# A fused four-layer kernel: one decay matrix in the state-space stage, and another order of transposes in the last attention stage

## The reference, cut to what matters

```python
dt = jax.nn.softplus(dt + dt_bias)
xBC = jax.nn.silu(conv3(xBC))                       # x: 512 columns, B and C: 64 each
dA = jnp.exp(dt * -jnp.exp(A_log))                  # per token and head
h = h * dA_t[:, :, None, None] + dBx_t              # both directions
y = einsum('bhpn,bn->bhp', h, C_t)
y = shift(y_fw) + shift(y_bw) + x_og * (x_og @ fcD_w.T + Dp)
```

```python
q, k = q * cos + rotate_half(q) * sin, k * cos + rotate_half(k) * sin
att = softmax(causal(q @ k.T / sqrt(32)))
x = x + (att @ v) @ wo.T
probs = softmax(rmsnorm(x) @ router_w.T); tp, ti = top_k(probs, 2)
```

## Time and profile before

| | |
|---|---|
| median of 3 runs | 3548.52 us (3543.6 to 3556.27) |
| profiled execution | 3556.74 us, of which the span is 3555.0 us |
| mean granted TensorE clock | 0.89 |
| busy, share of the span | PE 77%, PEld 61%, DVE 65%, ACT 48%, POOL 27% |
| stage `ffn2` | from about 1429 us to 2225 us |
| stage `att3` | from about 2702 us to 3175 us |

### The profile page before, as it was taken

How to read it: one execution, slowest core, us unless ns; L and a number is a source line. 1 busy time by engine, 2 the same in 40 slices (tenths; PEclk the granted TensorE clock), 3 DMA queues, 4 the chain that set the end, 5 groups by cost and what they waited for, 6 DMA issues and landing times. The chain is left out here.

```text
span 3555.0 us, 69418 instructions
## 1 busy us (share of the span) xinstructions
PE 2741.3 (77%) x19770; PEld 2158.8 (61%) x19770; DVE 2322.4 (65%) x6747; ACT 1718.7 (48%) x4856; POOL 942.4 (27%) x908
## 2 busy tenths in 40 slices
PE   3999947973849608799999998688885777739993
PEld 2777737973749607566666666456552445429993
DVE  5777745647755575577777775688883767734555
ACT  1434415645636427444444442566662555516664
POOL 0232343650533414011111111000001233333442
PEclk9999978986869858899999998899996989859997
DMA  5121102324212232000000000100001000002225
GB/s 177 53 67 54 55 24 80 86 82 165 77 47 61 60 108 87 1 1 0 0 0 0 0 0 1 33 19 18 24 12 55 13 19 21 22 31 55 66 60 166
DMA packets 142549, 168.57 MB, mean 47 GB/s; under 512 B 19920, under 2 KB 118224, under 8 KB 141776
## 3 DMA queue, kind: packets, MB, share of 16 engines
q1 hardware_dynamic: 117744, 120.77, 11.3%
q0 software_dynamic: 21504, 44.74, 3.6%
q10 hardware_dynamic: 3168, 1.49, 0.2%
HBM read 115.87 MB, written 51.05 MB: 47 GB/s over the span
## 5 line engine op out<-in xcount | busy, mean ns | idle before, releaser
L1145 POOL DMA_INDIRECT y_rows<-ffn_e_rows_out,ffn_e_scatter_at x352 | 341.2, 969 | 435.5 <-DVE ffn_e_rows_out L1173 251.7
L1286 PE MATMUL bank<-ffn_e_xT,ffn_e_mine 128*128 128x128 f32 x3360 | 438.5, 278 | 2.2 <-ACT ffn_e_xT L1219 1.4
L1286 PEld LDWEIGHTS bank<-ffn_e_xT,ffn_e_mine 128*128 128x128 f32 x3360 | 409.2, 194 | 3.4 <-ACT ffn_e_xT L1219 2.2
L889 POOL DMA_INDIRECT sorted_rows<-ffn_r_h,ffn_r_slot x320 | 317.9, 994 | 320.3 <-issue 320.3
L1221 ACT ACTIVATE ffn_e_mine<-constants 128x512 f32 (+1 forms) x352 | 250.2, 712 | 126.2 <-issue 78.2
L1193 DVE TENSOR_TENSOR ffn_e_hid<-ffn_e_act,bank 128x256 f32<-128x256 f32 (+1 forms) x280 | 136.1, 486 | 224.0 <-ACT ffn_e_act L1246 185.5
L1296 PE MATMUL bank<-ffn_e_mine,ffn_e_hid 128*128 128x128 f32 x1968 | 278.1, 276 | 2.4 <-DVE ffn_e_hid L1197 2.1
L1296 PEld LDWEIGHTS bank<-ffn_e_mine,ffn_e_hid 128*128 128x128 f32 x1968 | 247.5, 192 | 5.4 <-DVE ffn_e_hid L1197 5.0
L2469 ACT ACTIVATE gnn_prob<-bank,gnn_low 128x256 f32<-128x256 f32 x512 | 193.9, 490 | 52.8 <-DVE gnn_low L2387 52.8
L2387 DVE TENSOR_REDUCE gnn_low<-bank 128x2 f32<-128x512 f32 x256 | 159.0, 683 | 63.6 <-PE bank L2563 63.5
L2575 PE MATMUL bank<-ident,gnn_prob 128*128 128x128 f32 x1024 | 146.2, 278 | 42.2 <-DVE gnn_probT L2398 31.7
(11 more groups left out here) (502 smaller groups left out, 6782.4 us busy)
## 6 DMA issues: line engine op xcount, KB each, us to landing
g_adj<-in_adjT SPq DMA_DIRECT2D x48, 512.0 KB, 3.9
ffn_e_rows_in<-sorted_rows SPq DMA_DIRECT2D x346, 66.0 KB
ffn_c_y<-y_rows SPq DMA_DIRECT2D x80, 256.0 KB, 3.3
g_adj_rows<-in_adj SPq DMA_DIRECT2D x16, 512.0 KB, 4.2
gnn_adj<-in_adjT SPq DMA_DIRECT2D x16, 512.0 KB, 3.8
constants<-in_ffn SPq DMA_DIRECT2D x1, 6281.0 KB, 17.8
y_rows<-ffn_e_rows_out,ffn_e_scatter_at POOLq DMA_INDIRECT x352, 2.2
constants<-in_ffn SPq DMA_DIRECT2D x1, 5206.0 KB, 15.9
```

Source lines behind the costliest of these rows:

```text
L889: g.indirect_dma_start(self.c.sorted_rows, bass.IndirectOffsetOnAxis(self.slot[par][:, k, j:j + 1], 0), self.h[par][:, j, :], None).then_i ...
L1145: g.indirect_dma_start(c.y_rows, bass.IndirectOffsetOnAxis(scatter_at[par][:, k:k + 1], 0), rows_out[par][:, k, :], None).then_inc(scatter ...
L1286: ins = pe.matmul(chunk(part, ch), chunk(weights[:, i * HALF:(i + 1) * HALF], ch), x, start=True, stop=True)
```

## The change

In `ffn2`: B and C are projected by one group of four products with 128 output rows, and their taps run on 128 partitions (`bc` is one tile, taps moved ahead of the softplus chain). The decay is multiplied in one matrix for both directions: `dt_run` (dt times the mask; the forward half by eight ScalarE copies, the backward half by one VectorE product of 1024 columns), `dt_both` (their sum), `g_both` (the two triangles of B.C added) and `factor` (their product). The exponential is taken head by head with minus A as its scale. The output takes 8 products with `xtok`. GpSimd no longer makes `a_run` and `xdt`, and its addition of the output bias waits for `norm_ps`. The logit pieces 2 and 3, the transposes, the four pieces of `tail_fin` (`fin_piece`) and the residual have other places.

In `att3`: the eight transposes are dealt out between other products on TensorE; the router's logits and ranks move to unused columns of bank 7, `PV[:, 320:384]` and `PV[:, 256:320]`; and the steps of all engines stand in another order. ScalarE's order now: the copy of hT, the exponentials of the first quad with its transpose 2 before the last of them, the copy of the outputs of quad 0, the router's rows, the rows of h, the router's exponential, the outputs of quad 1, v, and the exponentials of the second quad with transpose 2, the copy of onT and the router's hT between them.

```diff
+
+                    g.wait_ge(norm_ps, t * 2 + 1)
...
-                        g.wait_ge(dt_ready, t + 1)
...
-                        g.tensor_tensor(heads(xdt[d][:]), heads(xtok[:]), per_head(dt[:, d * HEADS2:(d + 1) * HEADS2], HD2),
...
+                    g.wait_ge(xtok_ready, t + 1)
...
+                    if more:
+                        soft_a(t + 1, 2)
                     tap_more(0, xpad, conv_x, xc, range(KC)).then_inc(xc_ready, 1)
+                    then(v, tap_last(bcpad, conv_bc, w["convb_bc"], bc, range(1)), conv, t * 4 + 3)
+                    then(v, tap_more(1, bcpad, conv_bc, bc, range(1)), conv, t * 4 + 4)
+                    tap_more(0, bcpad, conv_bc, bc, range(1)).then_inc(bc_ready, 1)
...
+                    v.tensor_tensor(dt_run[1][:], per_head(dt[:, HEADS2:2 * HEADS2], P),
+                                    masks[:, 1, None, :].broadcast_to([P, HEADS2, P]), ALU.mult).then_inc(dt_back_ready, 1)
+                    v.wait_ge(dt_fwd_ready, t + 1)
+                    v.wait_ge(dt_back_ready, t + 1)
+                    v.tensor_tensor(dt_both[:], dt_run[0][:], dt_run[1][:], ALU.add).then_inc(dt_both_ready, 1)
...
+                    v.tensor_tensor(g_both[:], gm[:, 0, :], gm[:, 1, :], ALU.add).then_inc(g_both_ready, 1)
+                    v.wait_ge(g_both_ready, t + 1)
+                    v.wait_ge(dt_both_ready, t + 1)
+                    v.tensor_tensor(factor[:], dt_both[:], g_both[:, None, :].broadcast_to([P, HEADS2, P]), ALU.mult).then_inc(factor_ready, 1)
+                    if more:
+                        soft_b(t + 1, 1 - par, 2)
+                    v.wait_ge(factor_ready, t + 1)
...
-                        for d in range(2):
-                            v.tensor_tensor(decay[2 * d + half][:], B[6 + half][:].rearrange("p (a n) -> p a n", a=4),
-                                            gm[:, d, None, :].broadcast_to([P, 4, P]), ALU.mult).then_inc(decay_ready, 1)
-                    if more:
-                        soft_a(t + 1, 2)
-                        soft_a(t + 1, 3)
-                        soft_b(t + 1, 1 - par, 2)
+                        v.tensor_tensor(decay[half], B[6 + half][:].rearrange("p (a n) -> p a n", a=4),
+                                        factor[:, half * 4:half * 4 + 4, :], ALU.mult).then_inc(decay_ready, 1)
+                    if not first:
+                        residual(t - 1)
...
+                    if more:
+                        exp_piece(t + 1, 2)
...
+                    a.wait_ge(dt_ready, t + 1)
+                    for hd in range(HEADS2):
+                        ins = a.activation(dt_run[0][:, hd, :], masks[:, 0, :], ACT.Copy, scale=dt[:, hd:hd + 1])
+                    ins.then_inc(dt_fwd_ready, 1)
+                    swT_piece(t, 1)
+                    a.wait_ge(xt_ps, t + 1)
+                    a.activation(xtok[:], B[5][:], ACT.Copy).then_inc(xtok_ready, 1)
+                    if more:
+                        exp_piece(t + 1, 3)
                     for half in range(2):
                         a.wait_ge(D_ps, t * 2 + half + 1)
-                        a.activation(B[6 + half][:], B[6 + half][:], ACT.Exp).then_inc(D_exp, 1)
-                    a.wait_ge(xt_ps, t + 1)
-                    a.activation(xtok[:], B[5][:], ACT.Copy).then_inc(xtok_ready, 1)
-                    swT_piece(t, 1)
-                    if more:
-                        exp_piece(t + 1, 2)
-                        exp_piece(t + 1, 3)
+                        for k in range(4):
+                            one = B[6 + half][:, k * P:(k + 1) * P]
+                            ins = a.activation(one, one, ACT.Exp, scale=neg_a[:, half * 4 + k:half * 4 + k + 1])
+                        ins.then_inc(D_exp, 1)
...
+                    if more:
+                        lg_piece(t + 1, 2)
                     if not first:
                         tail_p(t - 1, more)
-                        tail_fin(t - 1)
+                    if more:
+                        lg_piece(t + 1, 3)
+                    if not first:
+                        fin_piece(t - 1, 0)
...
-                    pe.wait_ge(bcd_ready, t + 1)
-                    decays(0)
+                    if not first:
+                        fin_piece(t - 1, 1)
+                    swT_piece(t, par, 1)
+                    if not first:
+                        fin_piece(t - 1, 2)
...
+                    pe.wait_ge(bcd_ready, t + 1)
+                    pe.wait_ge(dt_fwd_ready, t + 1)
+                    pe.wait_ge(dt_back_ready, t + 1)
...
                     swT_piece(t, par, 2)
-                    pe.wait_ge(decay_ready, t * 4 + 4)
-                    pe.wait_ge(xdt_ready, t * 2 + 2)
+                    if not first:
+                        fin_piece(t - 1, 3)
+                    pe.wait_ge(xtok_ready, t + 1)
                     for hd in range(HEADS2):
-                        for d in range(2):
-                            ins = mm(B[5][:, hd * HD2:(hd + 1) * HD2], decay[2 * d + hd // 4][:, hd % 4, :],
-                                     xdt[d][:, hd * HD2:(hd + 1) * HD2], start=(d == 0), stop=(d == 1))
+                        if hd % 4 == 0:
+                            pe.wait_ge(decay_ready, t * 2 + hd // 4 + 1)
+                        ins = mm(B[5][:, hd * HD2:(hd + 1) * HD2], decay[hd // 4][:, hd % 4, :], xtok[:, hd * HD2:(hd + 1) * HD2],
+                                 start=True, stop=True)
                     ins.then_inc(y_ps, 1)
...
     WIDTH = 384
-    ACT_T = ((0, 1), (0, 3))
...
-        route = Route(nc, c, "ffn3", c.moe, ctx, M1, M1, M1)
+        route = Route(nc, c, "ffn3", c.moe, ctx, M1, PV[:, 320:384], PV[:, 256:320])
...
-                    scores_low(t, 0)
                     T(0, 0)
                     if since(t, 2):
                         route.vector_stats(v, t - 2, two)
+                    scores_low(t, 0)
+                    T(0, 1)
+                    if since(t, 2):
+                        route.vector_shift(v, t - 2, par, two)
+                    if not last:
+                        rope_q(t + 1, 1 - par)
+                    T(0, 3)
                     if since(t, 3):
                         route.vector_second(v, t - 3, three)
-                    T(0, 1)
                     if not last:
-                        rope_q(t + 1, 1 - par)
-                    T(0, 2)
+                        rope_k(t + 1, 1 - par)
+                    T(1, 0)
                     if since(t, 3):
                         route.vector_chosen(v, t - 3, three)
-                    if since(t, 2):
-                        route.vector_shift(v, t - 2, par, two)
-                    T(0, 3)
-                    if not last:
-                        rope_k(t + 1, 1 - par)
                     scores_low(t, 1)
-                    T(1, 0)
+                    T(1, 1)
+                    if not first:
+                        norm_o(t - 1, 1 - par)
                     if since(t, 3):
                         route.vector_places(v, t - 3, 1 - par, three)
-                    T(1, 1)
-                    if not first:
-                        norm_o(t - 1, 1 - par)
-                    T(1, 2)
-                    if since(t, 3):
                         route.vector_gates(v, t - 3, three)
                     T(1, 3)
+                    if not first:
+                        new_rows(t - 1)
                     if since(t, 2):
                         route.vector_first(v, t - 2, par, two)
-                    if not first:
-                        new_rows(t - 1)
...
+                    T(0, 0)
                     scores(t, par, 0)
-                    if not first:
-                        product_v(t - 1, 1 - par, 0)
                     if not last:
                         to_features(t + 1)
-                    T(0, 0)
                     T(0, 1)
                     if not last:
                         q_proj(t + 1)
                     T(0, 2)
+                    if not first:
+                        product_v(t - 1, 1 - par, 0)
                     T(0, 3)
                     if not last:
                         k_proj(t + 1)
                     scores(t, par, 1)
+                    T(1, 0)
                     if not first:
                         product_v(t - 1, 1 - par, 1)
                     if not last:
                         v_proj(t + 1)
-                    T(1, 0)
+                    T(1, 1)
...
                     T(1, 2)
+                    if not first:
+                        tokens_T(t - 1, last)
                     if since(t, 2):
                         pe.wait_ge(on_ready, t)
                         route.tensor_hT(pe, t - 2, par)
-                    if not first:
-                        tokens_T(t - 1, last)
                     T(1, 3)
+                    if not first:
+                        final(t - 1)
                     if since(t, 2):
+                        if since(t, 3):
```

(3 more changed lines are left out.)

135 lines of the change are left out of this document (60 added, 75 removed).

## The result

| | median | from to | ratio to before |
|---|---|---|---|
| before | 3548.18 us (4 runs) | 3543.6 to 3556.27 | |
| changed | 3414.35 us (4 runs) | 3411.13 to 3415.47 | 0.9619 [0.96, 0.9638] |

The kernel is 134 us faster; 95 were forecast. The profiled execution took 3411.13 us, 145.6 less than that of before. The traces place the gain: the first row minimum of the stage after ffn2 comes at 2144.5 for 2249.2, of which 104.0 arose in ffn2; the loop of att3 is 36.7 shorter, and its tail 1.7.

A forecast was written before the change was run, and what follows sets the result against it. TensorE was taken to bind ffn2, and waits handed between TensorE and VectorE to bind att3. Gains of 68 and 27 us, 95 in all, took 3548.52 to 3453 us; range 3413 to 3495 for 8 in 10.

The forecast's parts named there:

- The waits of ffn2: TensorE in ffn2: 3.92 us a turn of waits for GpSimd's tiles go, 2.5 new ones come, 1.4 gained.
- The products taken away: TensorE in ffn2: half the B/C products (0.98 us) and half the output products (1.88) go, 2.86 us a turn.
- The slack around the decay chain: ffn2: the factor, between the B/C products and the output product, is done about 1 us before it is needed.
- The ring of att3: att3: slots, indirect DMAs, landing, shift, rope_q, k products, back to slots: 23.0 us, 24.1 a turn with lower clock.
- Some turns have a stretch at the lower clock ... I leave them as frequent as they are.: ffn2: low-clock stretches, as the four decay products after the waits (3.5 us at 0.52), stay as frequent.
- The sum for ffn2: ffn2: 4.3 us a turn gained over fifteen turns, 65, plus perhaps 3 in the first turn: 68 us.
- att3: 27 forecast: att3: 1.8 us a turn in twelve turns, 21, plus 6 in the three turns before the first dispatch.
- Rival 1: att3: DMAs land before VectorE comes to the shift, so no ring, 21.5 us a turn; 3421 us, chance 0.12.
- Rival 2: ffn2's waits only change names, the turn gains 2.86 us of work, att3 gives 10; 3492 us, chance 0.22.
- rival 3: ffn2: decay chain runs in series behind dt, 8.2 us exposed against 6.8 that can go; 3560 us, chance 0.04.
- rival 4: Whole kernel: no change to speak of, the two stages cancelling; 3548 us, chance 0.02.
- The rule weighed: ffn2: SBUF contention with GpSimd's term adds up to 1.0 us a turn to the factor, mostly in slack; left out.

The follow-up runs named there:

- the work put back: Changed kernel with the B/C products and the output products of ffn2 computed twice in the same place; 3694.79 us on the second chip, ratio to before 0.9644.
- ffn2 alone: New ffn2 with the old att3, an edit against the changed kernel; 3452.55 us, ratio to before 0.9729.
- the later shift: Changed kernel with att3's vector_shift put behind the router's second choice, ahead of rope_k; 3384.12 us (0.9532), again on a third chip 3385.36 us (0.9528).

## Why the prediction was right and wrong

**Right.** The direction, and the engine that binds each stage. The waits of ffn2 in sum: 2.5 forecast, 2.55 measured, so 1.4 against 1.45 gained; the wait for the copied piece 1.3 against 1.18, that for yg 0.9 against 1.26. The products taken away: from start to start, less the waits behind them, those of B and C gave 0.92 and the output product 1.95, together 2.87 for 2.86. The slack around the decay chain: a clean turn is no shorter with a faster factor. The ring of att3: 24.1 us a turn forecast, 23.72 measured, 2.4 against 2.1 of wait at L773, and 21.5 against 21.41 without it.

**Two readings that were off.** The forecast gave all 3.92 us of waits to GpSimd's tiles. Only 1.01 + 0.67 + 0.80 = 2.48 were; 0.53 were for the gated x (f_xT) and 0.81 for the copied piece (f_swT), a wait that did not go but grew to 1.18. As the one for f_xT went and wasn't counted apart, the sum still came out, which is in part luck. And the last group of the output product started at 2195.49, not at 2198.3: it ran at the lower clock and took 7.06 us, not 3.8. So fifteen turns took 714.2, 47.61 each, not 47.8.

**The step that failed: "Some turns have a stretch at the lower clock ... I leave them as frequent as they are."** They went from 12 in fourteen turns to 3. The fourteen stood 1.14 us above a clean turn before, 0.37 after: 0.77 a turn, 11 us, and another 3.3 in the last output product, 7.06 for 3.76. The forecast took the waits away and priced their idle time alone. That waits at the decay products bring low stretches is shown: with two of 0.9 and 0.6 put back there, 12 came, and with the wait ahead of the pooling product moved, the last 3 went. But their number isn't set by the waits alone: the work put back, with no wait added, doubled them from 3 to 6. What sets it stays open.

**The term that was sized too small: TensorE's busy time, 2.86 forecast, 3.88 measured.** This is the larger miss, 15 us in fifteen turns. The removed products gave their 2.87; the rest came from products that stayed. Before, the four decay products ran in three groups:

```profile
1758.40 1.12 PE L2268 MATMUL bank<-f_a_run,constants 128*128 128x512 f32 x2 [0.67 <-POOL f_a_run L1859]
...
1762.19 1.96 PE L2268 MATMUL bank<-f_a_run,constants 128*128 128x512 f32 x4
```

With the 1.10 of the earlier trace rows that is 4.18 in all; now they are one group of 3.68, so 0.5 went with the stops between them. The waits put back ahead of them agree in direction: one group cut into two cost 0.19 of busy time. The four transposed pieces take another 0.3 less, and the rest lies in differences of about 0.1 in several groups, which aren't ascribed.

The sum for ffn2 is 14 x 6.10 + 6.65 for the last turn + 7.4 for the first, where 3 was forecast, so 99.5; the other 4.5 of the 104.0 lie behind the start of the last output product, 3.3 of them the one at the lower clock. 68 were forecast. The 104.0 is that of two profiled executions; by the runs of ffn2 alone the part is worth 96 to 101.

**att3: 27 forecast, 36 to 37 measured.** The ring was right and the low clock in it was not. The forecast had the k products at the lower clock in two turns of three, since a stretch after a pause had 0.55; the stage had 0.96, with 6 low stretches in 12 turns, and the products took 1.13 and 1.02 after 2.42 us of waiting. That gain was partly spent on the train of DMAs, which took 9.44 for 8.93 since one of the eight issues took 1.48. The turn came out 0.4 shorter than forecast, 12 x 2.2 = 26.3 for 21, and the first three turns gave 9.5 for 6.

**Rivals.** Rival 1 (no ring) gave a time near the truth, 3421, for a wrong reason: the ring is there, and most of the missing gain was in ffn2 (36 us of it, and 10 in att3). Rival 2 (waits renamed, the turn at 45 or more) is ruled out by the turn of 41.67, rival 3 by the same and by a factor that can be 0.76 us shorter without a shorter clean turn, rival 4 (no change) by the total.

**The rule weighed.** The factor took 1.98 us beside GpSimd's term and 1.22 without it, so it was held by 0.76 us. In the trace it started at 1761.57, with 0.90 us of the term's 1.04 still to run. That a VectorE instruction with two inputs in SBUF contends with a GpSimd one that reads SBUF is what the section Who interferes with whom of the Trainium skill's page SBUF states; the trace agrees. The estimate by it was up to 1.0. That it falls into slack was right too: a clean turn stayed within 0.02 us.

## What to carry to other kernels

Where one engine binds, a wait ahead of its longest products can cost more than its length: here 1.49 us of waits cost 2.6 us a turn, in longer waits elsewhere, in restarts of a group and in clock. So price the clock and the wait together: when waits go from the bound engine, low-clock stretches can go with them, and their number is a term with bounds of its own, not one to leave as it is. Count them in each run, also where no wait was touched. When a step with a wait for a slow queue can stand at several places of an engine's order, put it as late as its consumer allows: the later shift was worth 28 us. And read one clean turn of each kernel apart from the mean turn, and leave the last turn out of the mean, or the causes can't be told apart.

## What was not expected of the hardware

- Waits of 0.86 and 0.63 us ahead of eight fp32 instructions of 512 columns took the granted clock of the loop from 0.99 to 0.97, whereas one wait of 2.42 us in att3 was followed by products at full speed. The length of a wait alone did not tell.
- With 2.6 us of products added and no wait, the pooling product behind one and the same wait (1.1 to 1.3 us) ran at full clock in one turn and partly at the lower in the next, turn about (3.67 and 5.39 us).
- In ten trains of the changed att3 one of the eight indirect DMAs took 1.47 or 1.48 us on GpSimd instead of 0.96; before, one took 1.42 and the others 1.23 at most.
- On one chip the same programs took 8% longer, with waits of 8.6 us a turn in att3 that have no releaser in the trace, while ffn2 kept its length (a loop of 607.6 us in both places). An edit that saved 28 us elsewhere saved nothing there in that stage.
